# An LSTM step whose four output chunks are summed in three groups (one, two, one) in place of two pairs, with the sums of the gates written to PSUM

## The chip, the cores and the metric

The kernel runs on one core of one Trainium2 chip. The metric is the device time of one execution in microseconds, lower is better. Times of kernels are medians of several runs.

## What is computed

The reference adds two residual layers to x (8 sequences, 512 steps, 512 channels). The first is an LSTM, and its steps follow one on the other:

```
a = xw_t + prev_h @ Wh                 # [8,512] @ [512,2048]; xw_t = x_t @ Wx + b
i, f, o = sigmoid(a[:, :H]), sigmoid(a[:, H:2H]), sigmoid(a[:, 2H:3H])
g = tanh(a[:, 3H:])
c = f * prev_c + i * g
h = o * tanh(c)                        # [8,512], goes into the next step
```

The second, on x + LSTM(x), is a four-tap convolution with a projection to 2 x 64 columns, a softplus and a tanh, a linear scan over the 512 steps with 64 states, and a projection back to 512 channels.

## The kernel before

**Number format.** h is kept as two fp16 parts (high, low), side by side in the tile `hz`, and Wh as two fp16 matrices `whi` and `wlo`. h is the stationary operand of TensorE (8 batch rows for each part), Wh the moving one. The 512 hidden units are four chunks of 128; chunk c of the output has 16 column blocks of 32 columns: j = 0..3 times the four gates. The four j go to the four 32-partition strips of PSUM, with one weight load and one matmul each, so a "set" in this text is four loads and four matmuls that run side by side (x4 in the rows).

**Two halves of a step.** `recA` (tile `rec[0]`) sums output chunks 0 and 1 with 16 stationary columns and 256 moving ones (line 562), `recB` (`rec[1]`) sums chunks 2 and 3 with 32 stationary columns (zeros beside h put the two chunks in different rows) and 128 moving ones (line 569). Input chunk k of h is needed for the k-th part of each sum: `recur(t, half, k)`.

**What follows a sum.** VectorE turns the 32x32 blocks (`open_`, lines 971 and 974), adds high and low rows into `pre` in SBUF (`add`, `add_o`, lines 980, 983, 987); ScalarE takes the tanh of all gates from `pre` (`gates`, `gate_o`, lines 851 and 861; sigmoids are made of tanh); VectorE makes the products and the cell (`product`, `cell`, lines 992 and 997); ScalarE takes tanh of the cell (`tanh_c`, line 866); VectorE writes the high part of h (`high`, line 1003), GpSimd the full h (line 488), and VectorE the low part (`low`, line 1009). The semaphore `s_h[q]` lets TensorE use half q of h. ScalarE also writes the next step's xw_t into the `rec` bank (`seeds`, line 777), on which the matmuls accumulate.

**Order.** All engines run lists that are written out in the code, in order. In a step TensorE does the recurrent sums, then `beside(t)`: pieces of the x projection (`x_project`, line 521, its bias on 505), the convolution (line 646), the small projection `y_u` (619), transposes (499, 659) and the output (666), handed out to the steps by a planner that runs when the program is built. VectorE and ScalarE too have a `beside(t)` after their part of the step. The order of the recurrent sums on TensorE is

```
recur(t, 0, 0); recur(t, 0, 1); recur(t, 1, 0, (0,))      # needs s_h[0]: input chunks 0 and 1
recur(t, 0, 2); recur(t, 0, 3); recur(t, 1, 0, (1,))      # needs s_h[1]: input chunks 2 and 3
recur(t, 1, 1); recur(t, 1, 2); recur(t, 1, 3)
```

Of the kernel before, what the change touches and what calls it, by code (L numbers as in the profile page):

```python
# [5 lines left out]
def lstm_ssm_kernel(nc: bass.Bass, x, cond, Wx, Wh, b, conv_b, Wp, bp, Ws, bs, A_log, dt_log, Wo, bo, out):  # L6
# [21 lines left out]
    HS = 4  # L28

# [5 lines left out]
    with ctx:  # L35
# [6 lines left out]
        def sem(name):  # L42
# [10 lines left out]
        seed = sb("seed", [128, 2, TS // 2, 2, 256])  # L53
        mask = sb("mask", [128, 2, 2])
# [24 lines left out]
        tr = [sb("tr0", [128, 2, G, 4, NB]), sb("tr1", [128, G, 2, 2, NB])]  # L79
        pre = [sb(f"pre{h}", [128, G, 2, NB]) for h in range(2)]  # L80

        act = [sb(f"act{h}", [128, G + 1, 2 * NB]) for h in range(2)]
        ifgate, gc = (act[0][:, 0:2, :], act[1][:, 2:4, :]), (act[0][:, 3:5, :], act[1][:, 1:5:3, :])
        prod = [sb(f"prod{h}", [128, 2, 2 * NB]) for h in range(2)]
        tc = [sb(f"tc{h}", [128, 2 * NB]) for h in range(2)]
        osc = [sb(f"osc{h}", [128, 2 * NB]) for h in range(2)]
# [11 lines left out]
        scratch = nc.dram_tensor("xw_rows", [2, KC, 128, 512], f32, kind="Internal").ap()  # L98
# [20 lines left out]
        s_os = [sem(f"s_os{q}") for q in range(2)]  # L119
        s_h32 = [sem(f"s_h32{q}") for q in range(2)]  # L120

        s_rec = [sem(f"s_rec{q}") for q in range(2)]
# [4 lines left out]
        s_tr = [sem(f"s_tr{q}") for q in range(2)]  # L127
        s_add = [sem(f"s_add{q}") for q in range(2)]
        s_prod = [sem(f"s_prod{q}") for q in range(2)]
        s_c = [sem(f"s_c{q}") for q in range(2)]  # L130
        s_hh = [sem(f"s_hh{q}") for q in range(2)]
        s_h = [sem(f"s_h{q}") for q in range(2)]
# [24 lines left out]
        WIDTH = (256, 128)  # L157

# [4 lines left out]
        wst = [seed[:, k, :, :, :].rearrange("p t q f -> p (t q f)") if k < 2 else  # L163
               wpk[:, 4 * k - 8:4 * k - 4, :, :].rearrange("p z c n -> p (z c n)") for k in range(KC)]

# [6 lines left out]
        def tile_bank(g, c):  # L172
            return (pw[0], pw[1], pu, po)[c] if g == 0 else pw[c % 2]
# [77 lines left out]
        def evacuates(t):  # L251
# [5 lines left out]
        NEAR_END = {LAST - 2: ([(0, 20, 4, 2), (20, 32, 14, 1)], 20, 26, 0.65),  # L257
                    LAST - 1: ([(0, 33, -3, 3), (33, 49, 8, 4), (49, 64, 12, 3)], 12, 17, 0.65),
# [68 lines left out]

        AHEAD = [(c, k, part) for c in range(2) for k in WX[:3] for part in range(3)]
# [37 lines left out]
        def first_seeds(eng, p, count):  # L366

            for j in range(4):
                own = slice(128 * j, 128 * j + 128)
                rows = slice(2 * NB * p, 2 * NB * p + 2 * NB)  # L370
                if count > 1:
                    eng.dma_start(seed[32 * j:32 * j + 2 * NB, 0, p, :, :].rearrange("r q (c f) -> r (q c) f", f=128)[:, 0:count, :],
                                  scratch[0, 0:count, rows, own].rearrange("c r f -> r c f")).then_inc(s_seed0[p], 16)
                else:
                    eng.dma_start(seed[32 * j + 2 * NB:32 * j + 4 * NB, 0, p, 1, 0:128],
                                  scratch[0, KC - 1, rows, own]).then_inc(s_seed0[p], 16)
# [4 lines left out]
        def _(sync):  # L381
# [4 lines left out]
            def rows_out(g, c):  # L386

                sync.wait_ge(s_wev, KC * g + c + 1)
                if c == 0 and g >= 2:
                    sync.wait_ge(s_seedin[1], 256 * (g - 1))  # L390
                    if g > 2:
                        sync.wait_ge(s_seedin[0], 256 * (g - 2))
                    else:
                        for p in range(1, TS // 2):
                            sync.wait_ge(s_seed0[p], 16 * 8)
                sync.dma_start(scratch[g % 2, c, :, :], xs[:, c, :]).then_inc(s_rows[c], 16)

            def rows_back(g, c, z):

                if c == 0:  # L400
                    if 2 * g + z >= 2:
                        sync.wait_ge(s_seed[1], TS * (2 * g + z - 1) - 2)
                    else:

                        sync.wait_ge(s_wlo, z + 1)
                sync.wait_ge(s_rows[c], 16 * (g + 1))
                back = scratch[g % 2, c, :, :].rearrange("(t q) (j f) -> j q t f", q=2 * NB, j=4)
                row, col = ((0, 128 * (c % 2)), (2 * NB * (c % 2), 0))[c // 2]
                for j in range(4):
                    sync.dma_start(seed[32 * j + row:32 * j + row + 2 * NB, z, :, c // 2, col:col + 128],  # L410
                                   back[j, :, TS // 2 * z:TS // 2 * z + TS // 2, :]).then_inc(s_seedin[z], 16)
# [81 lines left out]
        def _(pe):  # L493
# [223 lines left out]
            for t in range(END):  # L717
# [14 lines left out]
                if t == CB:  # L732
                    conv_bias()
# [543 lines left out]
```

## Time and profile before

| | us |
|---|---|
| median of 3 runs | 1887.65 (1887.31 to 1887.77) |
| profiled execution, span | 1887.5 |
| first recurrent matmul of the loop | 47.7 |
| last recurrent matmul | 1871.1 |
| TensorE busy | 1806.9 (96%) |
| VectorE busy | 1387.4 (74%) |
| ScalarE busy | 1120.3 (59%) |

The profiled execution is 0.15 us shorter than the median of the runs, so terms of the trace can be set beside the run times as they stand. The loop does 511 recurrent steps between the two matmuls of the table, about 3.57 us each. Matmuls are pipelined: the length of a matmul's row holds its way through the array, so the distance of two starts, not the length, says how long TensorE is taken. The same holds for VectorE and ScalarE in part: the next instruction starts before the row of the last one ends.

### The profile page before, as it was taken

What the parts mean: (1) busy time and instruction counts of PE and PEld (TensorE: products, weight loads), DVE (VectorE), ACT (ScalarE), POOL (GpSimd) and SP (SyncE); (2) the same over time, 40 slices, a digit from 0 to 9 for tenths busy, and PEclk for the clock granted to TensorE, in tenths of its full rate; (3) what the DMA queues carried; (4) which work ended last, traced back from release to release, by engine and by line L of the source; (5) the groups of instructions that cost most, each with busy time, mean ns of one, the idle gap of its engine ahead of it and who ended that gap; (6) DMA issues with size and microseconds to landing.
All of it is one profiled execution on the core that took longest, in us unless ns stands there. A gap on an engine that the chain in (4) does not pass through costs nothing.

```text
span 1887.5 us, 124428 instructions
## 1 busy us (share of the span) xinstructions
PE 1806.9 (96%) x52834; PEld 1418.6 (75%) x52834; DVE 1387.4 (74%) x7266; ACT 1120.3 (59%) x4565; POOL 340.0 (18%) x1544
## 2 busy tenths in 40 slices
PE   6888999999999999999999999999999999999987
PEld 3666777777777777777777777777777787888875
DVE  8787667777776777767777776777767777777776
ACT  5555565665655656566565655656556565656564
POOL 1111111111111111111111111111111111111111
PEclk9999999999999999999999999999999999999999
DMA  6111111111111111111111111111112111211110
GB/s 236 54 46 36 48 48 44 51 53 48 50 52 44 57 46 54 49 45 59 46 51 55 49 50 48 57 41 54 54 38 66 44 48 54 60 38 56 44 35 25
DMA packets 112292, 100.75 MB, mean 53 GB/s; under 512 B 20225, under 2 KB 86069, under 8 KB 110710
## 3 DMA queue, kind: packets, MB, share of 16 engines
q1 hardware_dynamic: 111448, 90.70, 15.8%
q8 instruction: 415, 6.80, 1.5%
q10 hardware_dynamic: 288, 2.10, 0.3%
q14 instruction: 141, 1.16, 0.2%
HBM read 50.77 MB, written 41.94 MB: 49 GB/s over the span
## 4 chain that ended last, share of the span: by engine, by line
PE 76%; ACT 9%; DVE 8%; issue 2%; POOL 2%; DMA 1%; SPq 0%; DVEq 0%; ACTq 0%
PE recA L562 28%; PE recB L569 17%; PE pw L521 13%; PE pbc L646 13%; ACT act L851 4%; DVE tr L974 4%; ACT recA L777 3%; DVE pre L983 2%; POOL h L488 2%; DVE hz L1009 2%; PE pw L505 1%; ACT tc L866 1%; PE pu L619 1%; PE po L666 1%; DMA wpk<-in_L_cond_Wh_dram 1%
## 5 line engine op out<-in xcount | busy, mean ns | idle before, releaser
L851 ACT ACTIVATE act<-pre 128x64 f32<-128x64 f32 (+1 forms) x1024 | 255.6, 250 | 709.5 <-DVE pre L983 701.8
L569 PE MATMUL recB<-wlo,hz 128*32 128x128 f16 x16352 | 577.0, 219 | 0.4 <-issue 0.3
L569 PE MATMUL recB<-whi,hz 128*32 128x128 f16 x16352 | 576.8, 219 | 0.2 <-issue 0.2
L562 PE MATMUL recA<-whi,hz 128*16 128x256 f16 x8176 | 515.3, 274 | 54.2 <-DVE hz L1009 46.0
L562 PE MATMUL recA<-wlo,hz 128*16 128x256 f16 x8176 | 511.9, 273 | 0.0
L569 PEld LDWEIGHTS recB<-whi,hz 128*32 128x32 f16 x16352 | 437.5, 97 | 10.0 <-issue 0.4
L569 PEld LDWEIGHTS recB<-wlo,hz 128*32 128x32 f16 x16352 | 437.5, 97 | 3.0 <-issue 0.7
L562 PEld LDWEIGHTS recA<-whi,hz 128*16 128x16 f16 x8176 | 199.9, 88 | 282.5 <-DVE hz L1009 264.4
L974 DVE STREAM_TRANSPOSE tr<-recA 128x256 f32<-128x256 f32 x512 | 230.2, 450 | 228.4 <-PE recA L562 227.2
L646 PE MATMUL pbc<-yt,wpk 128*128 128x256 f32 (+1 forms) x1216 | 332.6, 381 | 0.0
L488 POOL TENSOR_TENSOR h<-osc,tc 128x16 f32<-128x16 f32 x1024 | 228.2, 223 | 451.0 <-ACT tc L866 451.0
L482 POOL TENSOR_SCALAR osc<-act 128x16 f32<-128x16 f32 x512 | 104.8, 205 | 1075.7 <-ACT act L851 1075.7
L992 DVE SCALAR_TENSOR_TENSOR prod<-act 128x32 f32<-128x32 f32 x1024 | 196.6, 192 | 72.1 <-ACT act L851 2.9
L777 ACT ACTIVATE recA<-seed,mask 128x256 f32<-128x256 f32 x510 | 234.9, 461 | 1.6 <-DMA seed<-xw_rows 1.6
L1009 DVE TENSOR_TENSOR hz<-h,hz 128x16 f16<-128x16 f32 x1024 | 179.6, 175 | 71.6 <-POOL h L488 5.1
L521 PE MATMUL pw<-wxl,xh 128*128 128x512 f32 x496 | 224.3, 452 | 0.0
L521 PE MATMUL pw<-wxh,xh 128*128 128x512 f32 x496 | 219.7, 443 | 0.0
L1003 DVE TENSOR_TENSOR hz<-osc,tc 128x16 f16<-128x16 f32 x1024 | 177.8, 174 | 53.6 <-ACT tc L866 3.8
L866 ACT ACTIVATE tc<-act 128x16 f32<-128x16 f32 x1024 | 212.4, 207 | 7.8 <-DVE act L997 1.9
L521 PE MATMUL pw<-wxh,xl 128*128 128x512 f32 x496 | 216.1, 436 | 0.0
L646 PEld LDWEIGHTS pbc<-yt,wpk 128*128 128x128 f32 x1216 | 175.5, 189 | 49.9 <-issue 10.1
L562 PEld LDWEIGHTS recA<-wlo,hz 128*16 128x16 f16 x8176 | 200.1, 88 | 9.4
(162 smaller groups left out, 2120.7 us busy)
## 6 DMA issues: line engine op xcount, KB each, us to landing
xw_rows<-xs SPq DMA_DIRECT2D x128, 256.0 KB, 2.4
seed<-xw_rows SPq DMA_DIRECT2D x1008, 32.0 KB, 2.0
xn<-in_x_dram SPq DMA_DIRECT2D x32, 256.0 KB
out_dram<-ot SPq DMA_DIRECT2D x32, 256.0 KB, 3.1
seed<-in_L_cond_Wh_dram ACTq DMA_DIRECT2D x2, 1024.0 KB, 6.9
wpk<-in_L_cond_Wh_dram SPq DMA_DIRECT2D x2, 1024.0 KB, 12.1
wlo<-in_L_cond_Wx_dram SPq DMA_DIRECT2D x2, 1024.0 KB, 13.5
xs<-in_L_cond_Wx_dram SPq DMA_DIRECT2D x1, 1024.0 KB, 9.7
```

What stands on the lines that cost most here:

```text
L488: pool.tensor_tensor(h32[:, 2 * q:2 * q + 2, t % HS, :], osc[q][:, :].rearrange("p (c b) -> p c b", c=2), tc[q][:, :].rearrange("p (c b) - ...
L521: pe.matmul(out, xx[:, g % 2, k, :], wxm[w][:, k, c, :, :, :], start=first, stop=False)
L562: ins = pe.matmul(rec[0][32 * j:32 * j + 2 * NB, 0:256].rearrange("p (c f) -> p c f", c=2), h[:, 2 * NB:4 * NB], w[:, k, :, :].rearrange(" ...
L569: ins = pe.matmul(rec[1][32 * j:32 * j + 32, 0:128], h[:, 2 * NB * (1 - c):2 * NB * (1 - c) + 32], w[:, k, 4 * (2 + c) + j, :], start=Fals ...
L646: ins = pe.matmul(pbc[:, NB * (lo - a):NB * (hi - a)], wpk[:, k, c, :], yt[:, n % XR, c, NB * (lo + k):NB * (hi + k)], start=(j == 0), sto ...
L777: act_eng.activation(rec[q][:, 0:WIDTH[q]], seed[:, t // TS % 2, t % TS // 2, q, 0:WIDTH[q]], ACT.Copy, scale=mask[:, q, t % 2:t % 2 + 1]) ...
L851: act_eng.activation(act[q][:, q:G, :].rearrange("p g n -> p (g n)"), pre[q][:, q:G, :, :].rearrange("p g c b -> p (g c b)"), ACT.Tanh, sc ...
L866: act_eng.activation(tc[q][:, :], act[q][:, 4, :], ACT.Tanh, scale=0.5).then_inc(s_tc[q], 1)
L974: dve.transpose(tr[0][:, :, :, :, :].rearrange("p c g z b -> p (c g z b)"), rec[0][:, 0:256]).then_inc(s_tr[0], 1)
L992: dve.scalar_tensor_tensor(prod[q][:, :, :], ifgate[q], 1.0, gc[q], ALU.add, ALU.mult).then_inc(s_prod[q], 1)
L1003: dve.tensor_tensor(hb[t % 2][:, 2 * q:2 * q + 2, 0:NB], osc[q][:, :].rearrange("p (c b) -> p c b", c=2), tc[q][:, :].rearrange("p (c b) - ...
L1009: dve.tensor_tensor(hb[t % 2][:, 2 * q:2 * q + 2, NB:2 * NB], h32[:, 2 * q:2 * q + 2, t % HS, :], hb[t % 2][:, 2 * q:2 * q + 2, 0:NB], ALU ...
```

## The change

The four output chunks form three groups, `GROUPS = ((0,), (1, 2), (3,))`, each with its own PSUM bank, semaphores and tiles. The pair is summed as `recB` was. A single chunk is cut in two halves of 64 columns (two gates each), which are stacked in one strip: 32 stationary columns and 64 moving ones, two sets where there was a share of one. h becomes free in three parts, so the sums wait at three places. The adds write `pre` into the unused part of the group's PSUM bank, except for the o gate of the pair (`preo`, in SBUF). GpSimd makes the full h of groups 0 and 1, VectorE that of group 2 (`full`). To have banks for this, the transposes of x and `y_u` share one bank (`pxu`). Rows of xw go to DRAM and back in another layout: 12 reads of a half block in place of 16. Two of the planner's start slots near the end move.

```diff
+    GROUPS = ((0,), (1, 2), (3,))
...
-        pre = [sb(f"pre{h}", [128, G, 2, NB]) for h in range(2)]
+        preo = sb("preo", [128, 2, NB])
...
-        rec = [bank("recA"), bank("recB")]
+        rec = [bank(f"rec{q}") for q in range(Q)]
-        px = bank("px")
-        pu = bank("pu")
+        pxu = bank("pxu")
+        pre = [rec[q][:, WIDTH[q]:WIDTH[q] + WIDTH[q] // 2].rearrange("p (g n) -> p g n", g=G) for q in range(Q)]
...
+            def sums(h, c, w, k):
+
+                q, end = group_of[c], k == KC - 1
+                if WIDTH[q] == 128:
+                    for j in range(4):
+                        ins = pe.matmul(rec[q][32 * j:32 * j + 32, 0:128],
+                                        h[:, 2 * NB * (1 - row_of[c]):2 * NB * (1 - row_of[c]) + 32], w[:, k, 4 * c + j, :],
+                                        start=False, stop=end, skip_group_check=True)
+                    return ins
+                for s in range(2):
+                    for j in range(4):
+                        ins = pe.matmul(rec[q][32 * j:32 * j + 32, 0:64], h[:, 2 * NB * (1 - s):2 * NB * (1 - s) + 32],
+                                        w[:, k, 4 * c + j, 64 * s:64 * s + 64], start=False, stop=end, skip_group_check=True)
+                return ins
...
+                    pe.wait_ge(s_h[0], t + 1)
...
                     recur(t, 0, 0)
...
+                    recur(t, 1, 0)
+                    recur(t, 2, 0)
+                    pe.wait_ge(s_h[1], t + 1)
                     recur(t, 0, 1)
-                    recur(t, 1, 0, (0,))
                     recur(t, 0, 2)
-                    recur(t, 0, 3)
-                    recur(t, 1, 0, (1,))
                     recur(t, 1, 1)
                     recur(t, 1, 2)
+                    pe.wait_ge(s_h[2], t + 1)
+                    recur(t, 0, 3).then_inc(s_rec[0], 1)
+                    recur(t, 2, 1)
+                    recur(t, 2, 2)
                     recur(t, 1, 3)
+                    recur(t, 2, 3).then_inc(s_rec[1], 1)
...
+                    recur(t, 3, 0)
+                    recur(t, 3, 1)
+                    recur(t, 3, 2)
+                    recur(t, 3, 3).then_inc(s_rec[2], 1)
...
                     add(t, 0)
                     open_(t, 1)
                     product(t, 0)
-                    add(t, 1)
+                    add_gif(t)
                     cell(t, 0)
+                    open_(t, 2)
                     add_o(t)
                     product(t, 1)
+                    add(t, 2)
+                    cell(t, 1)
                     high(t, 0)
-                    cell(t, 1)
+                    product(t, 2)
                     low(t, 0)
+                    cell(t, 2)
                     high(t, 1)
                     low(t, 1)
+                    full(t, 2)
+                    high(t, 2)
+                    low(t, 2)
```

TensorE, the recurrent sums of one step, before: all of them stand between two pieces of `beside` (L499, L521). `recA` is chunks 0 and 1, `recB` chunks 2 and 3, `hz` is h.

```order
L521 MATMUL pw<-wxh,xh 128x512
L562 MATMUL recA<-whi,hz 16x256 x4
L562 MATMUL recA<-wlo,hz 16x256 x4
L562 MATMUL recA<-whi,hz 16x256 x4
L562 MATMUL recA<-wlo,hz 16x256 x4
L569 MATMUL recB<-whi,hz 32x128 x4
L569 MATMUL recB<-wlo,hz 32x128 x4
L562 MATMUL recA<-whi,hz 16x256 x4
L562 MATMUL recA<-wlo,hz 16x256 x4
L562 MATMUL recA<-whi,hz 16x256 x4
L562 MATMUL recA<-wlo,hz 16x256 x4
L569 MATMUL recB<-whi,hz 32x128 x4
```

Twelve more of the last kind and its `wlo` twin follow, up to 16 sets of `recB`. The same place of the changed kernel, up to the end of group 0 (`rec0` chunk 0, `rec1` chunks 1 and 2); x8 is two sets, one for each half of 64 columns:

```order
L578 MATMUL rec0<-whi,hz0 32x64 x8
L578 MATMUL rec0<-wlo,hz0 32x64 x8
L572 MATMUL rec1<-whi,hz0 32x128 x4
L572 MATMUL rec1<-wlo,hz0 32x128 x4
L572 MATMUL rec1<-whi,hz0 32x128 x4
L572 MATMUL rec1<-wlo,hz0 32x128 x4
L578 MATMUL rec0<-whi,hz0 32x64 x8
L578 MATMUL rec0<-wlo,hz0 32x64 x8
L578 MATMUL rec0<-whi,hz0 32x64 x8
L578 MATMUL rec0<-wlo,hz0 32x64 x8
L572 MATMUL rec1<-whi,hz0 32x128 x4
L572 MATMUL rec1<-wlo,hz0 32x128 x4
```

Then come two more sets of `rec1`, the last four of `rec0`, eight of `rec1`, and 16 sets of 64 columns of `rec2`. What was 8 sets of 256 columns and 16 of 128 is 32 sets of 64 columns and 16 of 128.

VectorE, one step, before (the digits are the halves):

```order
L974 STREAM_TRANSPOSE tr0<-recA 128x256
L983 TENSOR_TENSOR pre0<-tr0 128x2x4x8
L971 STREAM_TRANSPOSE tr1<-recB 128x128
L992 SCALAR_TENSOR_TENSOR prod0<-act0 128x32
L980 TENSOR_TENSOR pre1<-tr1 128x48
L997 SCALAR_TENSOR_TENSOR act0<-prod0 128x16
L987 TENSOR_TENSOR pre1<-tr1 128x16
L992 SCALAR_TENSOR_TENSOR prod1<-act1 128x32
L1003 TENSOR_TENSOR hz0<-osc0,tc0 128x2x8
L997 SCALAR_TENSOR_TENSOR act1<-prod1 128x16
```

Three more (line 1009, 1003, 1009) end the step. And in the changed kernel (the digits are the groups):

```order
L1000 STREAM_TRANSPOSE tr0<-rec0 128x64
L1005 TENSOR_TENSOR rec0<-tr0 128x2x2x8
L1000 STREAM_TRANSPOSE tr1<-rec1 128x128
L1020 SCALAR_TENSOR_TENSOR prod0<-act0 128x16
L1011 TENSOR_TENSOR rec1<-tr1 128x48
L1025 SCALAR_TENSOR_TENSOR act0<-prod0 128x8
L1000 STREAM_TRANSPOSE tr2<-rec2 128x64
L1015 TENSOR_TENSOR preo<-tr1 128x16
L1020 SCALAR_TENSOR_TENSOR prod1<-act1 128x32
L1005 TENSOR_TENSOR rec2<-tr2 128x2x2x8
L1025 SCALAR_TENSOR_TENSOR act1<-prod1 128x16
L1037 TENSOR_TENSOR hz0<-osc0,tc0 128x8
```

Eight more follow (products and cell of group 2, and high, low and full parts of h), so VectorE has 20 instructions in a step where it had 13, and three of its adds have `rec` as output.

## Rows read from the trace of the kernel before

**Rows 1.** The page: share of the span for each engine, and granted clock.

```profile
PE 1806.9 (96%) x52834; PEld 1418.6 (75%) x52834; DVE 1387.4 (74%) x7266; ACT 1120.3 (59%) x4565; POOL 340.0 (18%) x1544
...
PEclk9999999999999999999999999999999999999999
```

**Rows 2.** Timeline of one step, TensorE: start us, us, operation.

```profile
901.49 0.29 PE L562 MATMUL recA<-whi,hz 128*16 128x256 f16 x4
...
901.93 0.23 PE L569 MATMUL recB<-whi,hz 128*32 128x128 f16 x4
...
902.65 0.23 PE L569 MATMUL recB<-wlo,hz 128*32 128x128 f16 x4
902.81 1.13 PE L646 MATMUL pbc<-yt,wpk 128*128 128x256 f32 x4
903.59 0.58 PE L521 MATMUL pw<-wxl,xh 128*128 128x512 f32 x1
904.02 0.40 PE L521 MATMUL pw<-wxh,xh 128*128 128x512 f32 x1
904.45 0.29 PE L562 MATMUL recA<-whi,hz 128*16 128x256 f16 x4
...
905.02 0.29 PE L562 MATMUL recA<-whi,hz 128*16 128x256 f16 x4
```

**Rows 3.** Timeline of the same step, VectorE, ScalarE and GpSimd.

```profile
902.15 0.45 DVE L974 STREAM_TRANSPOSE tr<-recA 128x256 f32<-128x256 f32 x1 [0.19 <-PE recA L562]
...
902.64 0.22 DVE L983 TENSOR_TENSOR pre<-tr 128x64 f32<-128x64 f32 x1
...
902.90 0.26 ACT L851 ACTIVATE act<-pre 128x64 f32<-128x64 f32 x1 [1.14 <-DVE pre L983]
902.93 0.32 DVE L971 STREAM_TRANSPOSE tr<-recB 128x128 f32<-128x128 f32 x1
...
903.18 0.19 DVE L992 SCALAR_TENSOR_TENSOR prod<-act 128x32 f32<-128x32 f32 x1
...
903.29 0.20 DVE L980 TENSOR_TENSOR pre<-tr 128x48 f32<-128x48 f32 x1
...
903.51 0.17 DVE L987 TENSOR_TENSOR pre<-tr 128x16 f32<-128x16 f32 x1
903.53 0.24 ACT L851 ACTIVATE act<-pre 128x48 f32<-128x48 f32 x1
...
903.80 0.19 DVE L992 SCALAR_TENSOR_TENSOR prod<-act 128x32 f32<-128x32 f32 x1
...
904.03 0.18 DVE L997 SCALAR_TENSOR_TENSOR act<-prod 128x16 f32<-128x16 f32 x1
...
904.24 0.22 ACT L866 ACTIVATE tc<-act 128x16 f32<-128x16 f32 x1
...
904.54 0.23 POOL L488 TENSOR_TENSOR h<-osc,tc 128x16 f32<-128x16 f32 x1 [0.35 <-ACT tc L866]
...
904.79 0.18 DVE L1009 TENSOR_TENSOR hz<-h,hz 128x16 f16<-128x16 f32 x1
```

**Rows 4.** Timeline of another step, TensorE at the end of its side work.

```profile
1516.40 0.40 PE L521 MATMUL pw<-wxl,xh 128*128 128x512 f32 x1
1516.73 0.29 PE L562 MATMUL recA<-whi,hz 128*16 128x256 f16 x4
```

**Rows 5.** Line 562 alone: duration min/median/max in ns, first and last start.

```profile
L562 PE MATMUL recA<-whi,hz x8176: 269/273/277, 47.7 to 1871.0; 128*16 128x256 f16 x200
```

**Rows 6.** VectorE groups by form: busy us, mean ns of one.

```profile
L1056 DVE TENSOR_TENSOR sp<-acc,sp 64x1 f32<-64x1 f32 x2 | 0.3, 152 | 0.1
...
L1041 DVE TENSOR_TENSOR smC<-smC,pbc 64x1 f32<-64x1 f32 x1 | 0.2, 159 | 0.0
```

**Rows 7.** ScalarE groups by form.

```profile
L768 ACT ACTIVATE xs<-pw 128x128 f32<-128x128 f32 x126 | 33.3, 264 | 0.0
...
L787 ACT ACTIVATE sg<-av 64x128 f32<-64x128 f32 x2 | 0.6, 310 | 0.1
```

More of the change, by code:

```diff
@@ L364, in tiles_done, with scratch_of, seed_rows @@
             return [(g, c) for g, c, k, part in project_at[t] if (c, k, part) == last_of(g, c)]
[L366 to L376, printed above, removed]
+        def scratch_of(g, q):
+            return scratch[g % 2, 65536 * GROUPS[q][0]:65536 * (GROUPS[q][-1] + 1)].rearrange("(s t r f) -> s t r f", s=8, t=TS, r=2 * NB)
+        def seed_rows(eng, g, q, z, p):
+            return eng.dma_start(seed[:, z, p, OFF[q]:OFF[q] + WIDTH[q]],
+                                 scratch_of(g, q)[:, TS // 2 * z + p, :, :])
         block = ctx.enter_context(nc.Block())
@@ L498, in x_transpose @@
                         pe.wait_ge(s_xev, g)
-                ins = pe.transpose(px[:, 128 * k:128 * k + 128], xn[:, g % 2, 128 * k:128 * k + 128], ident[:, :])
+                    if g >= 2:
+                        pe.wait_ge(s_wev, KC)
+                        before = sum(u_when[i][0] < x_base(g) for i in range(NP))
+                        if before:
+                            pe.wait_ge(s_usb, before)
+                ins = pe.transpose(pxu[:, 128 * k:128 * k + 128], xn[:, g % 2, 128 * k:128 * k + 128], ident[:, :])
                 if k == KC - 1:
@@ L574, in first_rows, with recur @@
-            def first_rows(t, half):
-                for j in range(4):
-                    own = slice(128 * j, 128 * j + 128)
-                    if half == 0:
-                        pe.matmul(rec[0][32 * j:32 * j + 2 * NB, 0:256].rearrange("p (c f) -> p c f", c=2),
-                                  dz[t][:, 2 * NB:4 * NB], xs[:, 0:2, own], start=(t == 1), stop=False, skip_group_check=True)
+            def recur(t, c, k):
+                for w in (whi, wlo):
+                    ins = sums(hz[(t - 1) % 2][:, k, :], c, w, k)
+                return ins
@@ L581, in first_rows @@
+            def first_rows(t, c):
+                q, first = group_of[c], t == 1 and row_of[c] == 0
+                for j in range(4):
+                    if WIDTH[q] == 128:
+                        pe.matmul(rec[q][32 * j:32 * j + 32, 0:128],
+                                  dz[t][:, 2 * NB * (1 - row_of[c]):2 * NB * (1 - row_of[c]) + 32],
+                                  xs[:, c, 128 * j:128 * j + 128], start=first, stop=False, skip_group_check=True)
                         continue
-                    for c in range(2):
-                        pe.matmul(rec[1][32 * j:32 * j + 32, 0:128], dz[t][:, 2 * NB * (1 - c):2 * NB * (1 - c) + 32],
-                                  xs[:, 2 + c, own], start=(t == 1 and c == 0), stop=False, skip_group_check=True)
+                    for s in range(2):
+                        pe.matmul(rec[q][32 * j:32 * j + 32, 0:64], dz[t][:, 2 * NB * (1 - s):2 * NB * (1 - s) + 32],
+                                  xs[:, c, 128 * j + 64 * s:128 * j + 64 * s + 64],
+                                  start=(first and s == 0), stop=False, skip_group_check=True)
@@ L586, in first_step @@
             def first_step():
-                for q in range(2):
+                for q in range(Q):
                     pe.wait_ge(s_h[q], 1)
@@ L595, in first_step @@
                         pe.wait_ge(s_dz, 2)
-                        for half in range(2):
-                            first_rows(0, half)
+                        for c in range(KC):
+                            first_rows(0, c)
                     for k in range(KC):
@@ L706, in _ @@
             pe.wait_ge(s_zeros, 1)
-            for q in range(2):
-                pe.matmul(rec[q][:, 0:256], ident[:, :], tr[0][:, :, :, :, :].rearrange("p c g z b -> p (c g z b)"),
-                          start=True, stop=True)
+            for q in range(Q):
+                pe.matmul(rec[q][:, 0:WIDTH[q]], ident[:, :],
+                          tr[1][:, 0:WIDTH[q] // 32, :, :, :].rearrange("p a c z b -> p (a c z b)"), start=True, stop=True)
             pe.wait_ge(s_max, KC + 2)
@@ L1187, in _ @@
             dve.wait_ge(s_first, 5)
-            for q in range(2):
+            for q in range(Q):
                 dve.sem_inc(s_h[q], 1)
```

296 lines of the change are left out of this document (148 added, 148 removed).

## The prediction

> **What bounds the kernel now.** The page comes first: TensorE is busy for 96% of the span, VectorE for 74%, ScalarE for 59%, and the granted clock of TensorE is 9 tenths or more in all slices, the level of 2.4 GHz [rows 1]. From this TensorE seems to be the bound, but its rows hold the way through the array. So the timeline of one step is read next, by starts. The reader is to see two things in it.
>
> First, TensorE's own work. Four sets of 256 columns take from 901.49 to 901.93, 0.11 us each; 13 distances of 128-column sets from 901.93 to 902.65 give 0.055 us each [rows 2]. A step has 8 and 16 of them: 0.88 + 0.89 = 1.77 us. The side work starts at 902.81, which is 0.10 us after the last set has streamed (902.65 + 0.055). Its last matmul starts at 904.02. In a step where nothing else holds TensorE the first recurrent matmul follows 0.33 us after such a start [rows 4], so here TensorE would be ready at 904.35; it starts at 904.45 [rows 2]. TensorE needs 1.77 + 1.64 = 3.41 us in this step and gets 3.54.
>
> Second, the loop that sets the 3.54. I follow the wait at 905.02 back (input chunk 2 of the next step; the same place of this step is 901.49, 3.53 us earlier) [rows 2, 3]: `recA` takes its last 4 sets (0.44) and `recB` 14 sets, the last starting at 902.65; 0.28 later the transpose of `recB` (902.93), 0.36 later its add (903.29), then tanh of the gates (903.53), product (903.80), cell (904.03), tanh of the cell (904.24), GpSimd's h (904.54), low part (904.79), and 0.23 later TensorE. Each start follows the end of the one before by 0.03 to 0.08 us. So the step is bound by this chain of latencies, and TensorE's side work fills the time behind it with 0.10 us to spare. Rows 4 show that there are steps without spare.
>
> Over the whole loop: (1870.1 - 47.7) / 510 = 3.573 us for a step, where 1870.1 is the last step's first matmul, some 0.9 us before the last start of the line [rows 5]. The 0.04 us over 3.54 are the heavier steps and single delays. The remaining 65 us (start and end) I leave as they are; the profiled execution's 1887.5 us is 0.15 below the median.
>
> **The change on TensorE.** From 128 to 256 columns a set grows by 0.11 - 0.055 = 0.053 us, so one of 64 columns would take 0.055 - 0.027 = 0.029, an estimate, with streaming as the bound. 16 + 16 such sets (groups 0 and 2) are 0.93 us, in place of 0.88 for the eight wide ones; group 1 is 0.89 as before. Recurrent work: 1.82 us, +0.05. The bounds for a 64-column set: 0.029, if it streams; 0.055, if loading or issuing four weight tiles and four matmuls is what takes 0.055 now, since a 128-column set has the same eight instructions. I take 0.029, as the starts in the rows grow in the ratio of columns (0.055 to 0.11) with nothing left over. Everything behind it on the queue moves: at 0.055 the recurrent work is 2.65 us.
>
> The Trainium skill ("TensorE: Matmul & The Clock Gate", section Back-to-back issue gap) gives about 60 cycles of 2.4 GHz, 25 ns, as the least distance for 1 to 64 columns. By that rule a set would still be 29 ns if the floor holds for each strip, and the sum is the same; if it held for each matmul whatever its strip, a set would be 100 ns, and the 55 ns that four of them take now [rows 2] speak against that.
>
> **The change on the loop.** The new critical loop goes through all three groups, since VectorE keeps its order. In us, from the start of input chunk 1's share of `rec0`: 8 sets of 64 and 4 of 128 columns and the last set of `rec0` starting 3 sets further, 0.23 + 0.22 + 0.09; end of its row and wait 0.24 (0.28 for 128 columns, 64 columns less) = 0.78. Transpose of 64 columns 0.25 (0.45 at 256, 0.32 at 128) + 0.035: 1.07. Add 0.185 (0.22 at 64 wide, 0.17 at 16) + 0.035: 1.29. Gates of group 0, 32 wide: 0.22 from SBUF (between 0.26 and 0.20), from PSUM 0.18, + 0.03: 1.50. Product 0, after which VectorE goes on 0.11 later, or 0.10 for the narrower one: 1.60. Add of group 1 0.20 + 0.035: 1.84. Gates 0.205 + 0.035: 2.08. Product 1: 0.11, 2.19. Add of group 2: 0.22, 2.41. Its gates: 0.21, 2.62. Product 0.175 + 0.035: 2.83. Cell, next VectorE start 0.08 later: 2.91. `high` of group 1, 0.175 + 0.035: 3.12. `low` 0.175 + 0.055 to TensorE: 3.35 [rows 2, 3].
>
> The price of PSUM in this sum: a ScalarE copy from PSUM takes 264 ns where a SBUF source of the same width takes 310 [rows 7]; I take 40 ns off the gates. For a VectorE output in PSUM no row exists. The nearest is one with an input there: 159 ns against 152 [rows 6], so I take nothing. Bounds: 0.04 us faster, as on ScalarE, or slower by half of such an instruction (0.07).
>
> So the loop falls by 0.18 us, 3.53 to 3.35. But TensorE's demand in the same step rises to 1.82 + 1.64 = 3.46 us, and that is now the larger one. **The bound passes from the chain to TensorE.** Light steps stop at the loop, heavier ones are longer, and single delays remain; VectorE's side work has less room, as seven more instructions at 0.1 us of start distance each stand in a step. For all this I put 0.06 in place of the 0.04 of before. Step: 3.52. 510 x (3.573 - 3.52) = 27 us off: **1860**.
>
> Costed at nothing: the narrower seeds and gate instructions of ScalarE (12 in a step where 8 were; ScalarE is 59% busy and waits each step for the add of the first group: more than 1 us before 902.90 [rows 3]); the smaller pieces to and from DRAM (they are asked for eight steps, 8 x 3.5 = 28 us, before their use); the shared bank of transposes and `y_u` (they stand steps apart in the planner's list). GpSimd has one instruction as before for osc and two for h, and hides.
>
> **The rivals.**
>
> *Rival 1, small sets don't pay (slower).* A 64-column set takes longer than it streams, from weight loads or issue. For it: 8 instructions in 29 ns have no row, and the program fetched by TensorE nearly doubles. Against it: loads lie beside matmuls now. It decides from (3.573 - 3.52) / 32 = 1.7 ns a set, so at 31 ns. At 35 ns: 3.52 + 0.19, 1957; at 55 ns some 3.52 + 0.83: 2285.
>
> *Rival 2, VectorE pays for its PSUM output (slower).* Three adds stand on the loop; at 0.07 each the loop is 3.35 + 0.21 = 3.56, with the 0.06 3.62: 1887 + 510 x 0.05 = 1911. By the Trainium skill ("Perfetto Trace Analysis", section Optimizing Scalar/DVE Operations), data access costs VectorE about 125 ns in PSUM against 60 in SBUF, and ScalarE 51 against 93; by that the loop comes to 3.55. The ScalarE part agrees with 264 against 310 ns, the VectorE part not with 159 against 152 for an input; no row here has an output.
>
> *Rival 3, side work gives way (faster still).* If TensorE's side work closes up in the waits inside the sums, the loop stands: 3.35 + 0.05 = 3.40, 88 us off: 1800. Against it: side work is one block behind the last sum.
>
> *Rival 4, nothing.* Delays of VectorE (20 instructions in place of 13) or of program fetch eat the 0.05 us: 1885 to 1890.
>
> **Chances.** Forecast (1840 to 1883) 0.43, rival 3 0.12, rival 1 0.26, rival 2 0.09, rival 4 0.10. Faster than 0.2%, about what a measurement here can tell (3.8 us): 0.55; the same 0.09; slower 0.36. The range takes in most of rival 3 and of rivals 1 and 2 up to a set of 34 ns: 1812 to 1935; the forecast's own range is 1840 to 1883.
>
> **What would show it.** Starts of 64-column sets 29 ns apart; `rec` adds of 64, 48 and 32 elements at 0.19 to 0.20 us; gates of 32 at 0.18; most steps with the first recurrent matmul 0.33 us after the start of the last side matmul, as in rows 4, and the next h ready before it; a step of 3.45 to 3.55. The prediction is wrong if sets take over 31 ns, if the adds take 0.25, or if steps still wait for `low` with TensorE idle.

## The result, and the profile after

The changed kernel takes 3093.65 us (median of 4 runs, 3085.0 to 3102.62); the kernel before, run beside it, 1887.71 us (4 runs, 1887.31 to 1888.74). The ratio is 1.6386, 95% interval 1.6352 to 1.642. The prediction was 1860 us, faster. It was wrong by far and in its sign.

The page of the changed kernel, the lines that answer to [rows 1], and those on the program and the chain:

```profile
PE 2199.4 (71%) x102132; PEld 1757.1 (57%) x102132; DVE 1641.3 (53%) x10848; ACT 1270.0 (41%) x6611; POOL 347.2 (11%) x1544
...
PEclk9989899899999998998989999999999999989998
...
q8 instruction: 800, 13.11, 1.8%
...
PE 69%; issue 28%; DVE 2%; ACT 1%; DMA 0%; SPq 0%; POOL 0%; DVEq 0%; POOLq 0%; ACTq 0%
...
L578 PE MATMUL rec<-whi,hz 128*32 128x64 f16 x32704 | 858.7, 201 | 350.4 <-issue 337.4
L578 PE MATMUL rec<-wlo,hz 128*32 128x64 f16 x32704 | 857.7, 200 | 348.6 <-issue 347.8
```

TensorE has nearly twice the instructions, but is busy for a smaller share of the span than the 96% of [rows 1]: every engine is idle more. What grew in the chain is "issue", time in which an engine waits for nothing that the profile shows; before it was 2% of the chain. The table of waits names it again, on TensorE (engine, line, what it waited for: us in all, times, longest):

```profile
DVE tr L1000 <- PE rec L578: 1139.3, 776, 4.8
ACT act L877 <- DVE rec L1005: 997.1, 504, 7.8
PEld rec L578 <- issue: 838.0, 636, 3.2
PE rec L578 <- issue: 687.9, 440, 3.1
```

VectorE waits for TensorE, and TensorE's line 578, the matmuls and weight loads of the 64-column sets, waits in hundreds of stops of up to 3.2 us. The timeline shows one of them, and then sets of the same kind without one (start us, us, operation):

```profile
1500.81 0.25 PE L578 MATMUL rec<-wlo,hz 128*32 128x64 f16 x8
...
1500.87 0.23 PE L578 MATMUL rec<-whi,hz 128*32 128x64 f16 x6
...
1503.32 0.10 PEld L578 LDWEIGHTS rec<-whi,hz 128*32 128x32 f16 x2 [2.34 <-issue]
1503.32 0.21 PE L578 MATMUL rec<-whi,hz 128*32 128x64 f16 x2 [2.22 <-issue]
...
1505.67 0.23 PE L578 MATMUL rec<-whi,hz 128*32 128x64 f16 x8
...
1505.73 0.23 PE L578 MATMUL rec<-wlo,hz 128*32 128x64 f16 x8
...
1505.79 0.23 PE L578 MATMUL rec<-whi,hz 128*32 128x64 f16 x8
...
1505.85 0.24 PE L578 MATMUL rec<-wlo,hz 128*32 128x64 f16 x8
```

At 1505.67 to 1505.85 eight matmuls (two sets) start every 0.06 us: a set takes 29 ns, as predicted. But at 1500.87 TensorE stops in the middle of two such sets, after 6 of 8 matmuls that use the same part of h, and stands for over 2 us. In all the trace's TensorE records (matmuls, weight loads and waits), counted in order of their starts, 769 distances are over 0.5 us (1099 us together), and 607 of them lie at one and the same place in a count modulo 256. The line `q8 instruction` of the page has 800 packets of 16 KB; 102132 matmuls, as many weight loads and 678 records of its sequencer are 204942, 256 for a packet. So q8 brings TensorE's program, 256 instructions to a packet, and TensorE stands where one packet's instructions end. 3095 / 800 is one packet every 3.87 us. Before, 415 packets came in 1887.5 us, one in 4.55 us, and "issue" held recurrent matmuls and loads for 3 us in the whole run.

The start and length of each q8 packet in the trace fit this. Call the 256 instructions between two such places a block. A packet starts 1.27 us on average after TensorE has started a block, it takes 1.09 us, and the next block starts 1.44 us after its end: together 3.81 us in the steady part of the run. Of the 607 stops nearly all end 1.2 to 1.6 us after the end of a packet, and just one packet starts in each of the 799 whole blocks.

In instructions of a step (loads, matmuls and a few waits): 208 before, of which the recurrent sums are 24 sets of 8; 401 after, with 48 sets of 8.

### The profile page after: what moved, and what is told of

It is laid out like the page before. It is cut to its first block, busy times and chain, and to the rows that moved or that the text cites. A ratio compares the mean times of both kernels' runs of the same rounds, so it can differ in the third digit from the quotient of the medians.

```text
span 3095.0 us, 230074 instructions
## 1 busy us (share of the span) xinstructions
PE 2199.4 (71%) x102132; PEld 1757.1 (57%) x102132; DVE 1641.3 (53%) x10848; ACT 1270.0 (41%) x6611; POOL 347.2 (11%) x1544
## 4 chain that ended last, share of the span: by engine, by line
PE 69%; issue 28%; DVE 2%; ACT 1%; DMA 0%; SPq 0%; POOL 0%; DVEq 0%; POOLq 0%; ACTq 0%
PE rec L578 23%; PE rec L572 18%; PE pw L539 13%; PE pbc L656 11%; PE po L676 1%; PE pw L523 1%; PE pxu L629 1%; DVE tr L1000 1%; PE po L669 1%; PE pxu L517 1%; DMA wpk<-in_L_cond_Wh_dram 0%; ACT act L877 0%; PE pw L554 0%; DVE hz L1043 0%; DVE prod L1020 0%
## 5 line engine op out<-in xcount | busy, mean ns | idle before, releaser
L578 PE MATMUL rec<-whi,hz 128*32 128x64 f16 x32704 | 858.7, 201 | 350.4 <-issue 337.4
L578 PE MATMUL rec<-wlo,hz 128*32 128x64 f16 x32704 | 857.7, 200 | 348.6 <-issue 347.8
L1000 DVE STREAM_TRANSPOSE tr<-rec 128x64 f32<-128x64 f32 (+1 forms) x1536 | 417.4, 272 | 1247.7 <-PE rec L578 1139.3
L578 PEld LDWEIGHTS rec<-whi,hz 128*32 128x32 f16 x32704 | 638.7, 100 | 593.7 <-issue 445.1
L578 PEld LDWEIGHTS rec<-wlo,hz 128*32 128x32 f16 x32704 | 616.8, 100 | 391.2 <-issue 389.5
L877 ACT ACTIVATE act<-rec 128x32 f32<-128x32 f32 (+1 forms) x1536 | 310.6, 202 | 1199.6 <-DVE rec L1005 997.1
L572 PE MATMUL rec<-wlo,hz 128*32 128x128 f16 x16352 | 725.8, 232 | 70.4 <-issue 70.4
L572 PE MATMUL rec<-whi,hz 128*32 128x128 f16 x16352 | 725.4, 232 | 60.1 <-issue 59.6
L572 PEld LDWEIGHTS rec<-wlo,hz 128*32 128x32 f16 x16352 | 482.0, 103 | 86.5 <-issue 85.6
L572 PEld LDWEIGHTS rec<-whi,hz 128*32 128x32 f16 x16352 | 455.7, 103 | 67.1 <-issue 66.2
L803 ACT ACTIVATE rec<-seed,mask 128x64 f32<-128x64 f32 x1530 | 493.2, 322 | 0.8
L892 ACT ACTIVATE tc<-act 128x8 f32<-128x8 f32 (+1 forms) x1536 | 319.1, 208 | 3.5 <-DVE act L1025 2.5
```

Of the source, the lines that this page charges most:

```text
L572: ins = pe.matmul(rec[q][32 * j:32 * j + 32, 0:128], h[:, 2 * NB * (1 - row_of[c]):2 * NB * (1 - row_of[c]) + 32], w[:, k, 4 * c + j, :], ...
L578: ins = pe.matmul(rec[q][32 * j:32 * j + 32, 0:64], h[:, 2 * NB * (1 - s):2 * NB * (1 - s) + 32], w[:, k, 4 * c + j, 64 * s:64 * s + 64], ...
L803: act_eng.activation(rec[q][:, 0:WIDTH[q]], seed[:, t // TS % 2, t % TS // 2, OFF[q]:OFF[q] + WIDTH[q]], ACT.Copy, scale=mask[:, t % 2:t % ...
L877: act_eng.activation(act[q][:, 0:slots, :].rearrange("p g n -> p (g n)"), pre[q][:, 0:slots, :].rearrange("p g n -> p (g n)"), ACT.Tanh, s ...
L892: act_eng.activation(tc[q][:, :], act[q][:, 4, :], ACT.Tanh, scale=0.5).then_inc(s_tc[q], 1)
L1000: dve.transpose(tr[q][:, :, :, :, :].rearrange("p a c z b -> p (a c z b)"), rec[q][:, 0:WIDTH[q]]).then_inc(s_tr[q], 1)
```

## The experiments

The theory after the first look, A: TensorE's program arrives at no more than 256 instructions in about 3.9 us, and 401 a step are more than that. Rivals: B, the 64-column sets or the three groups cost time themselves; C, each further instruction costs a fixed time. The kernel before, run beside them, took 1888.61 us for experiments 1, 2, 3 and 7, 1888.04 for 4, 6, 8 and 10, and 1887.2 for 5 and 9. Ratios are against these.

**1. The split alone.** The kernel before; each 128-column set of `recB` as two of 64, nothing else (64 more matmuls and 64 more weight loads: 336 instructions a step).

```diff
+                for s in range(2):
                     for j in range(4):
-                        ins = pe.matmul(rec[1][32 * j:32 * j + 32, 0:128], ...
-                                        w[:, k, 4 * (2 + c) + j, :], ...
+                        ins = pe.matmul(rec[1][32 * j:32 * j + 32, 64 * s:64 * s + 64], ...
+                                        w[:, k, 4 * (2 + c) + j, 64 * s:64 * s + 64], ...
```

> The kernel before, with each 128-column set of recB cut in two sets of 64 columns (same weights, same strips, same sums). Nothing else of the change is in it: two halves, gate sums in SBUF. Columns streamed are as before; TensorE's instructions per step go from 208 (106320 in 511 steps) to about 336. Theory A (program fetch): TensorE's program comes in packets of 16 KB, 256 instructions, no faster than one in 3.4 to 3.9 us (800 packets in the changed kernel's 3095 us are 3.87 us each). Expected 336/256 = 1.31 packets a step, 5.0 us, 2560 to 2660 us in all, with idle stretches of TensorE put down to issue at one place in 256 instructions. Rival B (three groups, their waits or sums in PSUM cause the stalls): 1885 to 1900 us. Rival C (short sets cost more in the array, 55 ns a set): 32 sets in place of 16, +0.9 us a step, about 2300 us, spread evenly and without long idle stretches.

Measured: 2644.03 us (ratio 1.4003, 1.3975 to 1.4031), 671 packets, 3.94 us for each. The loop, the groups and VectorE are those of before, so the three groups aren't needed for the slowdown. Of 603 distances over 0.5 us between TensorE's starts 384 lie at one place in 256, as A says. Sets that are slow by themselves (B) aren't excluded by the time of this run.

**2. More instructions with wide sets.** The kernel before, each matmul of `recB` preceded by one more load of the same weights (272 instructions a step, all sets 128 or 256 wide).

```diff
+                    pe.ldweights(h[:, 2 * NB * (1 - c):2 * NB * (1 - c) + 32], tile_position=(0, 32 * j))
                     ins = pe.matmul(rec[1][32 * j:32 * j + 32, 0:128],
```

> The kernel before, with one more weight load (the same weights, same strip) ahead of each matmul of recB: 64 instructions more a step, 272 in all, no matmul and no column more. Theory A: 1.06 packets a step, 4.0 to 4.1 us, 2110 to 2180 us. Rival C (it is the short matmuls): the loads lie beside the matmuls or cost at most 14 ns a set, 16 sets, 0.22 us, most of it inside TensorE's spare: 1887 to 1950 us.

Measured: 2166.84 us (1.1476, 1.1447 to 1.1505), 543 packets, 3.99 us for each. No set is narrow here.

**3. The changed kernel with wide sets.** Each single chunk as one 128-column set (its upper and lower halves no longer stacked), so 128 matmuls a step.

```diff
-    WIDTH = [64 * len(cs) for cs in GROUPS]
+    WIDTH = [128 for cs in GROUPS]
+    N8 = [8 * len(cs) for cs in GROUPS]
...
```

What is left out fits the tiles, the adds and the rows in DRAM to this width.

> The changed kernel, but a single chunk isn't cut in halves: one set of 128 columns in place of two of 64, 128 matmuls a step in place of 192, all three banks 128 columns wide (transposes and seeds of the single groups become 128 wide, and the rows of a single chunk are written to DRAM twice). Three groups, three waits and sums in PSUM stay. Instructions of TensorE about 273 a step. Theory A: 1.07 packets a step at 3.77 to 3.87 us, 4.0 to 4.15 us, 2110 to 2190 us. Rival B (groups, waits, PSUM): stays near 3095. Rival C (64-column sets): the stalls go altogether, loop of about 3.45 us, 1830 to 1890.

Measured: 2168.87 us (1.1487, 1.1464 to 1.151), 543 packets, 3.99 us for each. Experiments 2 and 3 have different loops, sets, groups and VectorE programs, the same number of instructions and packets, and the same time to 2 us. That is what A says, and B doesn't. C would also give one time for both, with 64 more instructions each; the next two experiments are for it.

**4. and 5. The dose.** The kernel before with 16 and with 32 more weight loads a step, as in experiment 2 but for the first one or two input chunks only.

```diff
+                    if k == 0:      # k < 2 in the second
+                        pe.ldweights(h[:, 2 * NB * (1 - c):2 * NB * (1 - c) + 32], tile_position=(0, 32 * j))
```

> Kernel before with 16 extra weight loads a step on TensorE (for the first input chunk of the second half's sums; 64 gave 2167 us): 224 instructions a step in place of 208. Theory A (a limit on the rate of fetch, 3.99 us for 256 instructions as in the two runs at 2167 and 2169): 224/256 x 3.99 = 3.49 us a step, under the 3.57 that the step takes, so little change, 1887 to 1900. Theory B (each further instruction of TensorE costs in proportion, 279 us / 64 = 4.4 us for each a step): 1957. Theory C (the extra loads' own time, some 14 ns for four when they stand ahead of their matmuls, up to 0.055): 1888 to 1915.

> Kernel before with 32 extra weight loads a step on TensorE: 240 instructions a step (16 gave 1896 us, 64 gave 2167). Theory A (the program comes at no more than 256 instructions in 3.97 us while data is moved too): 240/256 x 3.97 = 3.72 us a step in place of 3.57, so 1887 + 510 x 0.15 = 1964; 1940 to 1975. Theory B (the loads cost in proportion to those of the run with 16, 0.5 us for each a step): 1905. Theory C (each costs as in the run with 64, 4.4 us): 2027.

Measured: 1896.34 us (1.0045, 1.0029 to 1.006) with 447 packets, and 1960.3 us (1.0392, 1.0356 to 1.0428) with 479. The page and two of its waits for 32 more loads:

```profile
PE 1837.4 (94%) x52834; PEld 1439.2 (74%) x69250; DVE 1387.8 (71%) x7266; ACT 1120.8 (57%) x4565; POOL 338.5 (17%) x1544
...
q8 instruction: 479, 7.85, 1.7%
```

```profile
PEld recB L571 <- issue: 43.5, 73, 1.5
PE recB L571 <- issue: 34.9, 69, 1.3
```

The first 16 loads cost 8 us, the next 16 64 us, and the next 32 (experiment 2) 207 us: 0.5, 4.0 and 6.5 us for each load a step. A cost in proportion (C) is excluded. It is a limit that is reached between 208 and 240 instructions a step. The forecast from the rate, 1964, was 4 us off, and that was partly luck. Its 3.97 us for 256 is near span over packets, in which the run's start and end are spread over the packets; in the loop alone experiments 2 and 3 have (2167 - 65) / 511 / 272 x 256 = 3.87 us, by which 240 instructions need 3.63 us, 1915 in all. So close to the limit a kernel pays more than the mean rate alone says. Why it does wasn't tested.

| kernel | instructions a step | packets | us | us from packet to packet |
|---|---|---|---|---|
| before | 208 | 415 | 1888 | 4.55 |
| + 16 loads | 224 | 447 | 1896 | 4.24 |
| + 32 loads | 240 | 479 | 1960 | 4.09 |
| + 64 loads | 272 | 543 | 2167 | 3.99 |
| changed, wide sets | 272 | 543 | 2169 | 3.99 |
| before, `recB` split | 336 | 671 | 2644 | 3.94 |
| changed | 401 | 800 | 3094 | 3.87 |

**6. Whose program.** The kernel before with 64 more instructions a step on SyncE, waits for a semaphore that has its value already.

```diff
             for t in range(END):
+                for z in range(64):
+                    sync.wait_ge(s_wlo, 1)
```

> Kernel before with 64 more instructions a step on SyncE (waits for a semaphore that has its value already), none on TensorE. The same number on TensorE gave 2167 us. Theory A (what is limited is the fetch of TensorE's own program, 256 instructions in 3.9 to 4.0 us): 1887 to 1895, TensorE's program 415 packets as before. Theory B (one shared limit for the programs of all engines): 2100 or more. Theory C (SyncE itself becomes late with its transfers, 64 waits of some 20 to 50 ns a step are 1.3 to 3.2 us of 3.57): still 1887 to 1900, since its transfers are asked for many steps ahead.

Measured: 1899.49 us (1.0058, 1.0043 to 1.0074). TensorE's packets stay at 415; another instruction queue grows from 141 to 270. The same number on TensorE costs 279 us, here 11, so the limit is not shared. The 11 us are above what A allowed and at the upper end of C's range (1887 to 1900): ScalarE waits for four seed transfers, 9.4 us together, so SyncE does come late with some.

```profile
ACT recA L779 <- DMA seed<-xw_rows: 9.4, 4, 6.2
```

**7. The changed loop without the limit, first try.** Experiment 3 with the low parts of the weights left out for the single chunks; 208 instructions a step.

```diff
-                for w in (whi, wlo):
+                for w in ((whi, wlo) if group_of[c] == 1 else (whi,)):
```

> As the run with one set a chunk, and the single chunks leave out the wlo part of their sums (the output has less precision in half of the units): 96 matmuls a step, as many as before; TensorE's instructions are about 209 a step. Theory A: 0.82 packets a step, 3.1 us at 3.8, so the fetch is no bound; the three-group loop shows itself: the sum of the prediction with 128-column transposes is about 3.43 us, so 3.45 to 3.52 a step, 1830 to 1865 us. Rival B: far above 1887, with the long idle stretches. The run also says what the three groups would be worth if their instructions were free.

Measured: 1935.11 us (1.0247, 1.023 to 1.0264), 416 packets. The stops at one place in 256 are gone (8 at the commonest place, where experiment 3 has 214), so far A. But 1935 is 70 us over what A with the predicted loop allowed: there is a second error, and it is in the loop.

**8. The changed loop with its 64-column sets.** The changed kernel, with the low parts of the weights left out of all recurrent sums after the first step: 96 matmuls a step.

```diff
-                for w in (whi, wlo):
+                for w in (whi,):
```

> Changed kernel, all three groups and the 64-column halves kept, but the low parts of the recurrent weights left out in every step after the first (so the recurrent sums lack them): 24 fewer sets, 96 matmuls and 96 weight loads a step, as many as before. Theory A (the whole slowdown is the rate at which TensorE's program arrives): no long stops at one place in 256 instructions. Its time is then that of the loop through the three groups. From the rows of the run with 128-column single chunks (3.56 us in the step at 901.56) minus 0.07 for each of two narrower transposes and 0.06 for shorter sets behind the last low part: 3.36, with the 0.10 by which that kernel's mean lies above this step 3.46, so 1825 to 1840 us. Theory A' (the loop was mis-sized by more than the transposes: waits between VectorE and ScalarE): 1900 to 1940. Theory B (64-column sets cost time by themselves): over 2000, with sets more than 31 ns apart.

Measured: 1907.57 us (1.0104, 1.0088 to 1.0119), 417 packets: no limit from the program, 24 sets fewer than the changed kernel, and still slower than before. The 1825 to 1840 expected was wrong too. The timeline of one step shows the loop:

```profile
900.46 0.24 DVE L1000 STREAM_TRANSPOSE tr<-rec 128x64 f32<-128x64 f32 x1
...
900.73 0.20 DVE L1005 TENSOR_TENSOR rec<-tr 128x32 f32<-128x32 f32 x1
...
902.36 0.22 POOL L502 TENSOR_SCALAR osc<-act 128x16 f32<-128x16 f32 x1
...
902.55 0.17 DVE L1025 SCALAR_TENSOR_TENSOR act<-prod 128x8 f32<-128x8 f32 x1
...
902.68 0.17 DVE L1037 TENSOR_TENSOR hz<-osc,tc 128x16 f16<-128x16 f32 x1
902.73 0.22 POOL L494 TENSOR_TENSOR h<-osc,tc 128x16 f32<-128x16 f32 x1
...
902.98 0.18 DVE L1043 TENSOR_TENSOR hz<-h,hz 128x16 f16<-128x16 f32 x1
903.07 0.16 DVE L1031 TENSOR_TENSOR h<-osc,tc 128x8 f32<-128x8 f32 x1
903.17 0.17 DVE L1037 TENSOR_TENSOR hz<-osc,tc 128x8 f16<-128x8 f32 x1
...
903.44 0.17 DVE L1043 TENSOR_TENSOR hz<-h,hz 128x8 f16<-128x8 f32 x1
...
903.67 0.12 PEld L578 LDWEIGHTS rec<-whi,hz 128*32 128x32 f16 x8 [0.22 <-DVE hz L1043]
...
903.97 0.25 DVE L1000 STREAM_TRANSPOSE tr<-rec 128x64 f32<-128x64 f32 x1
```

The step is 3.51 us. The predicted loop gives, from the first transpose (0.78 in its sum), 2.05 to the cell of group 2, 2.13 to `high` of group 1, 2.34 to `low`; the rows give 2.09, 2.22 and 2.52. The first 0.04 is spread. Of the rest 0.05 arises between cell and `high`; its cause isn't shown, and over all steps the median of this distance is the 0.08 of the prediction. 0.09 arises between `high` and `low` (0.08 in the median), where GpSimd's h (902.73 to 902.95) must come first and had no term. Then TensorE doesn't wait for that `low` alone: group 2's three instructions follow on VectorE, its low part starts 0.46 us later, and TensorE waits for that one at 903.67. From `low` of group 1 to the next transpose it is 0.99; by the predicted way, with the sets that this kernel has, it would be 0.23 + 0.12 + 0.11 + 0.03 + 0.24 = 0.73.

**9. The closing of the loop.** Experiment 8 with the full h of group 2 on GpSimd, as for the other groups.

```diff
                 full(t, 1)
+                full(t, 2)
...
-                    full(t, 2)
                     high(t, 2)
```

> The run with high parts only (1907.6 us, low parts of the recurrent weights still left out), and the full h of group 2 made on GpSimd, behind that of group 1, in place of VectorE. Theory A (the loop closes through the low part of group 2, which the prediction took as hidden behind the sums of chunks 1 and 2): in the step at 900.46 VectorE's full h starts at 903.07, the high part at 903.17, the low part waits for it and starts at 903.44, TensorE at 903.67. Without the full h on VectorE the high part starts at 903.07 and the low part at 903.28, GpSimd's h being done at about 903.23; 0.16 us a step, so 1820 to 1835 us. Theory B (the loop closes through the low part of group 1 and TensorE, as predicted): group 2 is off the path, no change, 1900 to 1908. Theory C (VectorE's work as a whole bounds it, 84% busy): 0.10 us a step for the instruction that it loses, 1855 to 1860.

Measured: 1860.55 us (0.9859, 0.9842 to 0.9877), 47 us under experiment 8, 0.092 us a step. The timeline of one step:

```profile
900.91 0.23 DVE L1001 STREAM_TRANSPOSE tr<-rec 128x64 f32<-128x64 f32 x1
...
903.40 0.18 DVE L1044 TENSOR_TENSOR hz<-h,hz 128x16 f16<-128x16 f32 x1
903.49 0.17 DVE L1038 TENSOR_TENSOR hz<-osc,tc 128x8 f16<-128x8 f32 x1
903.52 0.21 POOL L494 TENSOR_TENSOR h<-osc,tc 128x8 f32<-128x8 f32 x1
...
903.76 0.17 DVE L1044 TENSOR_TENSOR hz<-h,hz 128x8 f16<-128x8 f32 x1
...
904.28 0.25 DVE L1001 STREAM_TRANSPOSE tr<-rec 128x64 f32<-128x64 f32 x1 [0.35 <-PE rec L579]
```

From low to low it is 0.36 us in place of 0.46, and the step 3.37 in place of 3.51. B, no change, is excluded. But 1860.55 is 26 us above A's range and at the edge of C's (1855 to 1860), so the time fits VectorE's work as such (0.10 us a step) at least as well as the shorter path. How much each gives these two runs don't part: 0.14 in the step looked at, 0.092 on average. That TensorE waits for group 2's low part rests on the rows of experiment 8.

**10. The gate sums in PSUM alone.** The kernel before, with the outputs of its two adds in columns 256 to 320 of the recurrent banks.

```diff
-        pre = [sb(f"pre{h}", [128, G, 2, NB]) for h in range(2)]
+        preo = sb("preo", [128, 2, NB])
...
+        pre = [rec[h][:, 256:320].rearrange("p (g c b) -> p g c b", g=G, c=2) for h in range(2)]
```

> Kernel before with its gate sums (outputs of the two adds after the transposes) in PSUM beside the recurrent sums; the output gate's sum of the second half stays in SBUF. Two instructions of VectorE and two of ScalarE a step change their memory. TensorE's program stays at 208 instructions a step. Theory A (the changed kernel's rows: an add of 32 elements a partition with output in PSUM takes 0.20 us where 0.185 was estimated, ScalarE's gates from PSUM 0.03 to 0.04 us less): the chain loses about 0.025 us a step, 1870 to 1880 us. Theory B (VectorE pays 0.065 us for an output in PSUM): 1887 + 510 x 0.03 = 1900 to 1910. Theory C (TensorE's side work, 0.10 us behind the chain, is the real bound, or the rate at which its program comes): 1885 to 1890, no change.

Measured: 1876.61 us (5 runs, 1876.12 to 1879.01), ratio 0.9943, 0.993 to 0.9957: faster than both kernels. Groups by form of the kernel before (busy us, mean ns of one, idle before):

```profile
L851 ACT ACTIVATE act<-pre 128x64 f32<-128x64 f32 x512 | 131.2, 256 | 702.0 <-DVE pre L983 701.8
L851 ACT ACTIVATE act<-pre 128x48 f32<-128x48 f32 x512 | 124.5, 243 | 7.5 <-DVE pre L980 2.0
L983 DVE TENSOR_TENSOR pre<-tr 128x64 f32<-128x64 f32 x512 | 114.9, 224 | 17.6
...
L980 DVE TENSOR_TENSOR pre<-tr 128x48 f32<-128x48 f32 x512 | 103.7, 203 | 0.0
```

And of this experiment:

```profile
L984 DVE TENSOR_TENSOR recA<-tr 128x64 f32<-128x64 f32 x512 | 119.0, 232 | 17.6
L852 ACT ACTIVATE act<-recA 128x64 f32<-128x64 f32 x512 | 114.2, 223 | 712.7 <-DVE recA L984 712.7
L981 DVE TENSOR_TENSOR recB<-tr 128x48 f32<-128x48 f32 x512 | 111.0, 217 | 0.0
L852 ACT ACTIVATE act<-recB 128x48 f32<-128x48 f32 x512 | 107.1, 209 | 19.7 <-DVE recB L981 0.8
```

The output in PSUM costs VectorE 8 and 14 ns, the source in PSUM saves ScalarE 33 and 34 ns. The second half's pair stands on the chain of [rows 3]: 14 - 34 = -20 ns, times 510 is 10 us, of the 11.4 measured. Both pairs were changed at once, so that it was the second one is read from the chain and not from this run.

## Why the prediction was wrong

**What bounds the kernel now:** right as far as it went. A chain of latencies sets the step: 20 ns off the pair in it that experiment 10 changed gave 11 us. But the section listed two bounds, the chain (3.54) and TensorE's time (3.41), and there was a third close by. At the 3.87 us for 256 instructions of experiments 2 and 3, the 208 of a step need 3.14 us. The page had the count (415 packets of q8 in 1887.5 us), and the prediction didn't read it.

**"So one of 64 columns would take 0.055 - 0.027 = 0.029, an estimate, with streaming as the bound":** this term, and with it "Recurrent work: 1.82 us, +0.05", is the step that failed. As the length of a set in a burst 0.029 is right: the sets do start every 29 ns in the timeline (0.11 - 0.055 is 0.055 and not 0.053, which changes nothing). But the recurrent work was summed from such starts alone, with no term for bringing 384 instructions to the engine. At 3.87 us for 256 a set of 8 instructions takes 0.12 us, whatever its width; 401 instructions are 6.06 us a step by this, an estimate from the loop of experiments 2 and 3, against (3095 - 65) / 511 = 5.93 measured and 3.52 predicted. As a mean over a step the bounds 0.029 and 0.055 were both too low. Two of the signs that the prediction named for being wrong stayed silent in a kernel that was 64% slower: sets at 29 ns, not over 31, and adds at 0.20 to 0.21 us, not 0.25. The third, TensorE idle until `low`, showed with 144 us in 358 waits of its weight loads, a small part of the 1206 us.

**Rival 1** had the right cause beside a wrong one ("the program fetched by TensorE nearly doubles"), and priced only the wrong one, per set, up to 2285; rival 4 named program fetch too, for 0.05 us at most. The observation that "a 128-column set has the same eight instructions" and takes 0.055 was taken as a ceiling. It is none: at 0.055 a set the 256 instructions of a packet last 1.8 us, and the next packet comes after 3.8 or more. Before, the 24 wide sets of a step were 192 instructions, less than a packet, and the side work, 1.64 us with 16 instructions, gave the next one time to arrive. A burst shows the engine, the mean over a step shows the supply.

**The loop, 3.35:** wrong as well, shown by experiments 7 and 8, and hidden in the changed kernel by the first error. Up to `low` of group 1 it is 0.18 us too short (2.34 for 2.52), and half of that is GpSimd's h, which the prediction put at nothing ("GpSimd has one instruction as before for osc and two for h, and hides"). Its end, through the sums of chunks 1 and 2 with group 2's low part covered, held only on paper: in experiment 8 group 2's low part is what TensorE waits for. In the changed kernel the sums before it are twice as long, so less shows: 0.46 + 0.23 to chunk 3's sums, 0.30 as in the rows and 0.06 for two more sets are 1.05, against 1.01 in the prediction. That makes 3.35 + 0.18 + 0.04 = 3.57 for the loop, or 3.52 without the 0.05 whose cause isn't shown, an estimate, against 3.53 before. So without the program's limit the changed kernel would hardly have been faster either; experiment 8, with half its recurrent sums, took 1907.6. The full computation without the limit can't be run, as its instructions are what meets the limit.

**PSUM:** VectorE's output was put at nothing with a bound of +0.07; it is 0.008 and 0.014. ScalarE's gain was put at 40 ns and is 33 to 34. Rival 2 is out. By the Trainium skill ("Perfetto Trace Analysis", section Optimizing Scalar/DVE Operations) the output would have cost 65 ns, an estimate from its 125 ns for PSUM and 60 for SBUF. The 8 and 14 ns measured here disagree with it for an output of this form, while ScalarE's 33 to 34 ns less agree with its 42 (93 less 51) in sign and roughly in size.

**"Costed at nothing":** narrower seeds and gates, smaller transfers and the shared bank: the changed kernel's waits name no seed transfer in the loop, and the shared bank with 4.9 us in the whole run, where its forerunner had 4.7; beside the stops on the program little could have shown. Rival 3 was never reached.

## What to carry to other kernels

Count TensorE's instructions, weight loads too, over a step and divide by the step: the kernel before had 208 in 3.57 us, 17 ns for each. At 15.5 ns (experiment 5) it was already slower, and no kernel here, with its steps all written out as instructions, came below 14.8 ns on average, however short the single set looked in a burst. The page says how near one is: span over packets of TensorE's instruction queue, 4.55 us here when free and 3.9 to 4.0 when bound. Cutting a set in two for a shorter latency doubles its instructions; a narrower piece of the same work only pays where this budget has room. And when one group is made into three, follow the last group's closing instructions to the engine that waits too, since they come after those that one has in view.

## What the hardware showed that was not expected

- TensorE's program comes in packets of 16 KB for 256 instructions, and in the four bound kernels one came every 3.87 to 3.99 us on average. In the changed kernel's window of 1500.0 to 1506.5 us no data moves at all, and two instruction packets are the only DMA; TensorE stands for 2.34 us even so. So contention with data isn't needed for it. Nor is it the transfer alone, which takes 1.1 to 1.2 of the 3.8 to 3.9 us: in these four kernels a packet starts 1.2 to 1.35 us after TensorE has started a block of 256, and the next block starts 1.4 to 1.5 us after the packet's end. By these times one packet is fetched in each block and none ahead, and the limit is the time of such a round. Why no packet is fetched sooner was not found.

```profile
DMA packets 2, 0.03 MB, mean 5 GB/s; under 512 B 0, under 2 KB 0, under 8 KB 0
...
q8 instruction: 2, 0.03, 2.3%
```

- SyncE's program comes over another queue: 64 more instructions a step on it took q14 from 141 to 270 packets and left TensorE's q8 at 415.
- The granted clock fell with the stops: 0.919 of full speed in the changed kernel, 0.945 in experiment 1, 0.992 and 0.995 in experiments 2 and 3, against 0.996 before. The 0.919 is a mean of two levels: 1.2 GHz for 503 us, 16% of the span, and 2.4 GHz for the rest; shortly before each fall TensorE had stood still for 1.7 us or more. The lower clock lengthens the side matmuls (492 ns for one form against 445 in experiment 8), but isn't the cause: experiments 2 and 3 are slower by 15% at 0.99.
- In experiment 10 an add of VectorE with its output in PSUM takes 8 to 14 ns more than with SBUF, and a ScalarE activation that reads PSUM 33 to 34 ns less than one that reads SBUF.
